# Layer-norm tiles turned by VectorE's 32x32 blocks and a trip through DRAM, in place of TensorE transposes, in six passes of a two-layer network

## The reference

```python
x = x + 0.5 * ffn0(layernorm(x))      # silu(x W1^T) * (x W3^T), Walsh-Hadamard transform, W2; inner width 2048
x = x + attention(layernorm(x))       # a second layernorm inside, causal softmax, residual
x = x + 0.5 * ffn0(layernorm(x))
x = x + 0.5 * ffn1(layernorm(x))      # ternary weights, scaled; inner width 1408
x = x + state(layernorm(x))           # tanh(x B^T) C^T + D * x, inner width 256
x = x + 0.5 * ffn1(layernorm(x))
```

## Time and profile before

| | |
|---|---|
| median of 3 runs | 1705.29 us (1704.77 to 1708.26) |
| span of the profiled execution | 1703.6 us, 1.7 us under that median; no time of its own is given for it beside the span |
| PE, weight loads of PE | 99% and 82% of the span |
| VectorE, ScalarE, GpSimd | 68%, 49%, 7% |
| moved by DMA | 344.56 MB in 97341 packets |

### The profile page before, as it was taken

The page is one execution under the profiler, slowest core; times in us unless marked ns, Lnnn a source line. Parts: engine busy times, 40 slices in busy tenths (PEclk is TensorE's granted clock), DMA queues, the critical chain, the costliest instruction groups (busy, mean ns, idle before and its releaser), DMA issues.

```text
span 1703.6 us, 21742 instructions
## 1 busy us (share of the span) xinstructions
PE 1694.7 (99%) x7707; PEld 1401.8 (82%) x7707; DVE 1154.4 (68%) x1808; ACT 830.3 (49%) x1359; POOL 125.5 (7%) x185
## 2 busy tenths in 40 slices
PE   9999999999999999999999999999999999999998
PEld 7788888888888888888888888888888888888887
DVE  8888678677775555754446554447768869877866
ACT  5745444465575543434223333224556556655644
POOL 1000000000012220000000000000000143200001
PEclk9999999999999999999999999999999999999999
DMA  9776665699985000253444433444666763366765
GB/s 317 266 310 247 229 258 211 236 377 369 369 333 207 1 0 1 87 191 126 153 167 167 167 142 136 167 167 146 232 215 211 273 222 112 113 242 234 257 221 213
DMA packets 97341, 344.56 MB, mean 202 GB/s; under 512 B 10192, under 2 KB 25424, under 8 KB 91856
## 3 DMA queue, kind: packets, MB, share of 16 engines
q1 hardware_dynamic: 97232, 343.14, 55.0%
HBM read 261.83 MB, written 81.26 MB: 201 GB/s over the span
## 4 chain that ended last, share of the span: by engine, by line
PE 94%; DVE 3%; DMA 1%; SPq 1%; issue 1%; ACT 0%; DVEq 0%; ACTq 0%
PE psum L561 35%; PE psum L563 30%; PE psum L565 27%; PE psum L857 2%; DMA x<-in_w2a 1%; SPq L705 1%; DVE xc_lo L2074 0%; DMA flat<-in_w3a 0%; DMA w<-w_kept 0%; PE psum L1134 0%; DVE att_lo L2043 0%; DVE fw_lo L2037 0%; SPq L664 0%; DVE x L2020 0%; DVE x L2123 0%
## 5 line engine op out<-in xcount | busy, mean ns | idle before, releaser
L561 PE MATMUL psum<-xc_hi,w 128*128 128x512 f32 x1544 | 604.6, 392 | 0.5 <-DVE psum L2143 0.3
L563 PE MATMUL psum<-xc_lo,w 128*128 128x512 f32 x1544 | 600.9, 389 | 0.0
L565 PE MATMUL psum<-xc_hi,w 128*128 128x512 f32 x928 | 361.3, 389 | 0.0
L561 PEld LDWEIGHTS psum<-xc_hi,w 128*128 128x128 f32 x1544 | 289.8, 188 | 64.4 <-DVE psum L2143 1.6
L563 PEld LDWEIGHTS psum<-xc_lo,w 128*128 128x128 f32 x1544 | 289.9, 188 | 58.8
L561 PE MATMUL psum<-w,hid 128*128 128x512 f32 x864 | 337.5, 391 | 0.0
L565 PE MATMUL psum<-w,hid 128*128 128x512 f32 x864 | 336.4, 389 | 0.0
L2107 DVE TENSOR_TENSOR x<-psum,x 128x512 f32<-128x512 f32 x256 | 173.0, 687 | 148.3 <-PE psum L565 147.7
L563 PE MATMUL psum<-w,hid 128*128 128x512 f32 x544 | 211.7, 389 | 0.0
L565 PEld LDWEIGHTS psum<-xc_hi,w 128*128 128x128 f32 x928 | 174.2, 188 | 36.7
L2131 DVE TENSOR_TENSOR hid<-sg,hid 128x512 fp32r<-128x512 f32 x212 | 144.3, 691 | 85.2 <-ACT hid L1450 83.3
(11 more groups left out here) (177 smaller groups left out, 2030.1 us busy)
## 6 DMA issues: line engine op xcount, KB each, us to landing
w<-w_kept SPq DMA_DIRECT2D x93, 896.0 KB, 6.6
w<-w_kept SPq DMA_DIRECT2D x130, 512.0 KB, 7.1
w<-w_kept SPq DMA_DIRECT2D x57, 640.0 KB, 4.4
w_kept<-w SPq DMA_DIRECT2D x16, 1792.0 KB, 7.3
w<-w_kept SPq DMA_DIRECT2D x93, 256.0 KB, 4.5
w_kept<-prep SPq DMA_DIRECT2D x12, 1792.0 KB, 7.6
w_kept<-w SPq DMA_DIRECT2D x16, 512.0 KB, 6.3
w_kept<-prep SPq DMA_DIRECT2D x12, 512.0 KB, 8.9
```

The costliest lines, as they stand in the source:

```text
L561: pe.matmul(out, a_hi, b_hi, start=start, stop=False, skip_group_check=onto)
L563: last = pe.matmul(out, a_hi, b_lo, start=False, stop=stop and zero == "a", skip_group_check=onto)
L565: last = pe.matmul(out, a_lo, b_hi, start=False, stop=stop, skip_group_check=onto)
```

## The change

Six passes (`SWAPPED` = 0, 2, 3, 4, 5, 6) turn the tiles for their follower in another way. VectorE transposes a normalised tile in blocks of 32x32 (`swap_pair`) into `swap`, the two tiles of a pair interleaved. SP then stores `swap` to a scratch tensor in DRAM, one DMA for each group of 32 partitions, waits until all four have landed, and loads it back in four DMAs, which moves each block to its partitions of `xs` (`turn_load`). PE's transposes and ScalarE's copies of these passes go. Tokens of a pair now alternate in `xs` and in `hid`, so the downs of the passes fed in this way (1, 3, 4, 5, 7, and two chunks of the state stage) take every second column (`columns`). Attention's and the state stage's own transposes stay. Some sums move by a unit, and pass 6 normalises in units 4 to 7 in place of 4, 4, 5, 6.

```diff
-NORMS = {4: (3, 4, 5, 6), 5: (4, 5, 6, 7), 6: (4, 4, 5, 6), 7: ()}
+NORMS = {4: (3, 4, 5, 6), 5: (4, 5, 6, 7), 6: (4, 5, 6, 7), 7: ()}
+SWAPPED = (0, 2, 3, 4, 5, 6)
+BLOCK = 32
+LANDED = 16 * 4
...
+        def columns(no, i):
+            if no in (0, BEFORE_T, BEFORE_S):
+                return slice(i * P, (i + 1) * P)
+            return slice(i // 2 * 2 * P + i % 2, (i // 2 + 1) * 2 * P, 2)
...
                     w13_part(v, block, FIRST_W, w13_in)
+                if between:
+                    turn_load(*between)
                 if low_before:
...
+            def turn_load(ps, k):
+                c, cols = k // 2, k % 2 * 2 * P
+                sp.wait_ge(swapped, swaps_before(ps) + 2 * k + 2)
...
+                for a in range(P // BLOCK):
+                    sp.dma_start(turn_scratch[:, :, :, a, :].rearrange("i b k t -> i (b k) t"),
+                                 swap[a * BLOCK:(a + 1) * BLOCK, :, :, :, :].rearrange("p b k j i -> p (b k) (j i)")
+                                 ).then_inc(turn_stored[ps.no], 16)
+                sp.wait_ge(turn_stored[ps.no], (k + 1) * LANDED)
+                for b in range(P // BLOCK):
+                    sp.dma_start(xs[b * BLOCK:(b + 1) * BLOCK, 2 * c:2 * c + 2, :, cols:cols + 2 * P].rearrange("p h k t -> p (h k) t"),
+                                 turn_scratch[:, b, :, :, :].rearrange("i k a t -> i k (a t)")).then_inc(turn_in[ps.no], 16)
...
-                blocks, c, ts = ps.groups[g], i // TT, slice(i % TT * P, (i % TT + 1) * P)
+                blocks, c, ts = ps.groups[g], i // TT, columns(ps.no, i % TT)
...
-                    else:
-                        bank_free("n", n)
-                        pe.wait_ge(xn_ready, n + 1)
-                        turn(xn[:, tile % 4, :], plan.bank["n", n]).then_inc(turn_ready, 1)
...
+            def swap_pair(ps, k):
+                for j in range(2):
+                    dve.wait_ge(xn_ready, plan.norm_base[ps.no] + 2 * k + j + 1)
+                    if k:
+                        dve.wait_ge(turn_stored[ps.no], k * LANDED)
+                    nc.vector.transpose(swap[:, :, :, :, j], xn[:, j, :].rearrange("p (k b t) -> p b k t", k=KD, b=P // BLOCK)
+                                        ).then_inc(swapped, 1)
```

More of the change, by code:

```diff
@@ L193, in state_space @@
         self.s_unit, self.s_w2 = self.u, self.w2
-        self.s_downs, self.s_turn = [[] for _ in range(CH)], self.turn
+        self.s_downs, self.s_turn, self.s_norm = [[] for _ in range(CH)], self.turn, self.norm
+        self.norm += PT
         self.uses += -self.uses % 4
@@ L577, in w13_part, with w13_load @@
                 sp.dma_start(w13[:, v % 2, 0, cols].bitcast(F32), w13_kept[block][:, cols]).then_inc(landed[v % 2], 16)
-            def w13_load(v, block, second_before=None, with_low=True, low_before=False):
+            def w13_load(v, block, second_before=None, with_low=True, low_before=False, between=None):
                 if v < 2 * UNITS["A"]:
@@ L755, in _ @@
                     mix_split_out(MIX_IN.index(s))
+                if s in passes[0].norms:
+                    turn_load(passes[0], passes[0].norms.index(s))
                 if s + 1 in MIX_IN:
@@ L1064, in state_down @@
             def state_down(c, i, d):
[L1065 removed]
+                ts = columns("S" if c < 2 else BEFORE_S, i)
                 bank_free("d", d)
@@ L1941, in _ @@
             pool.wait_ge(skip_in, 16)
-            for n, tile in (tt for tiles in passes[BEFORE_S - 1].turns for tt in tiles):
+            for tile in range(PT):
                 if tile == 2:
                     chunk()
-                pool.wait_ge(turn_ready, n + 1)
-                skip(xn[:, tile % TT, :], x[:, tile, :], xn[:, tile % TT, :])
+                pool.wait_ge(swapped, swaps_before(passes[BEFORE_S - 1]) + tile + 1)
+                skip(xn[:, tile % 2, :], x[:, tile, :], xn[:, tile % 2, :])
             chunk()
@@ L2053, in sums @@
             def sums(ps, step):
-                b11, b12, b21, b22, t2 = (xs[:, n, :, :] for n in range(5))
+                b11, b21, b12, b22, t2 = (xs[:, n, :, :] for n in range(5))
                 if step == 0:
-                    dve.wait_ge(turned, turns_before(ps.no))
+                    dve.wait_ge(*all_turned(ps.no))
                     tt(b12, b22, b12, ALU.subtract).then_inc(sums_ready, 1)
@@ L2240, in up_slot @@
                         sums(following, 2 * (s - ps.n + 3) + step)
+                swapping = ps.no in SWAPPED and s in ps.norms
+                if swapping and ps.no:
+                    swap_pair(ps, ps.norms.index(s))
                 if not last:
@@ L2249, in up_slot @@
                     hid_low(u, 1)
+                    if swapping and ps.no == 0:
+                        swap_pair(ps, ps.norms.index(s))
                     hid_low(u, 0)
@@ L2344, in ternary_slot @@
                     return
-                if follower(ps) and s in FIRST_SUMS:
-                    sums(follower(ps), FIRST_SUMS[s])
+                if follower(ps):
+                    for step in FIRST_SUMS[ps.no + 1].get(s, ()):
+                        sums(follower(ps), step)
                 behind = bool(ps.downs[s]) and s not in ps.open
@@ L2359, in ternary_slot @@
                     extra(ps, s, k + 1)
-                if follower(ps) and s in LAST_SUMS:
-                    sums(follower(ps), LAST_SUMS[s])
+                if follower(ps):
+                    for step in LAST_SUMS[ps.no + 1].get(s, ()):
+                        sums(follower(ps), step)
+                if s in ps.norms:
+                    swap_pair(ps, ps.norms.index(s))
                 sum_c22(u)
```

103 lines of the change are left out of this document (58 added, 45 removed).

## The result

The changed kernel takes 1741.59 us, the median of 4 runs (1740.7 to 1743.8), against 1705.85 us for the kernel before in the same series. The ratio is 1.0209, 95% interval 1.0195 to 1.0224. It is slower by 2.1%, 35.7 us, where the prediction had 8 us.

A forecast was written before the change was run, and what follows sets the result against it. The prediction took TensorE, busy 1694.7 of 1703.6 us, as the only bound. It summed 1705.3 - 22.3 (transposes gone) + 30.4 (w2 stalls in passes 4, 5, 6) = 1713.4 us, range 1690 to 1757.

The forecast's parts named there:

- The gain, 22.3 us: PE's transposes in six passes: 24 pairs at 0.93 us each go, 22.3 us saved.
- the plain passes: Passes 0, 2, 3: SP reaches the next weights 3.6 us late, hidden; their 12 pairs keep 11.2 us.
- DVE's transposes, 0: Two transposes a pair on VectorE, 0.65 us each, were claimed to add 0 us.
- The cover of 0.4 us: In the unit ending at 1250.96, VectorE's gated product would still finish 0.4 us ahead of the unit's end.
- The cycle, 13.7 us: SP's queue in passes 4, 5, 6: weights 8.7, stores 2.6, landing 0.7, load issues 1.7, against a 9.97 us unit.
- Rival 2: 256-byte store rows are read before written, twice 28 ns a packet: cycle 18.3 us, total 1755; chance 0.12.
- The stalls, 30.4 us: PE waiting for late w2 in ternary passes: 10.7 each in passes 5 and 6, 9.0 in pass 4.
- the 2.0 a unit later: In pass 4, about 2 us more stall from what is left in the queue a unit later.
- A gap of several us may also lower the clock: Closing remark on PE's gaps: a lower clock would add to the loss; no size given.
- rival 3: Downs' stepped weight loads: twice 188 ns adds 150 ns each, 200 us, total 1910; decides from 227 ns; chance 0.06.
- the forecast span of 1711.7: Whole kernel: what the profiled execution's 1703.6 us span would become, 1.7 us below the forecast median.
- the rule of the Trainium skill: Partitions 0 to 31 reach 8 of 16 ports, 189 GB/s: a pair's eight transfers take 5.5 us, sum about 1726.

The follow-up runs named there:

- experiment 3: Changed kernel, but TensorE turns the tiles of passes 4, 5, 6 as before; tokens sorted where the operand is split: 1696.3 us, 0.9937 of the kernel before.
- 11: The kernel of experiment 3 (passes 0, 2, 3 alone through DRAM) measured again in another series: 1697.0 us, 0.9940 of the kernel before.
- 12: Changed kernel, but passes 4, 5, 6 turn only their first pair through DRAM, four places in xn, tokens sorted at the operand split: 1695.3 us, ratio 0.9931.
- experiments 4: Changed kernel, tokens sorted at the operand split, stores and loads of pairs in passes 4, 5, 6 issued on GpSimd's own queue: 1752.4 us, ratio 1.0257.
- 7: Changed kernel, but in passes 4, 5, 6 a pair's stores and loads queue behind the unit's w13 and w2 loads: 1738.5 us, ratio 1.0198.
- experiment 8: The kernel before, with TensorE held in eight units until GpSimd has run some small operations, making gaps: 1751.0 us, ratio 1.0266.
- experiment 1: Changed kernel, but the downs take 128 neighbouring columns in every pass, so no weight load is stepped: 1730.8 us, ratio 1.0138.
- experiment 9: Changed kernel, but TensorE turns the second and fourth pair in passes 4, 5, 6; tokens sorted at the operand split: 1701.3 us, ratio 0.9966.
- the sorted split: Changed kernel, a pair's tiles sorted apart where ScalarE and VectorE split the operand into xc_hi and xc_lo, avoiding stepped weight loads: 1735.0 us, ratio 1.0165.

## Why the prediction was wrong

- *The gain, 22.3 us, and the plain passes.* Right, to within 2 us in 11.2 (experiments 3 and 11). The last pair makes SP 4.1 us late for its weights (806.72 against 817.62 less 14.96; forecast 3.6), and the units are 14.96 us. SP's queue in pass 2, changed kernel:

```profile
806.72 0.91 SPq L599 DMA_DIRECT2D w<-w_kept  x2
...
817.62 0.80 SPq L599 DMA_DIRECT2D w<-w_kept  x2
...
832.58 0.80 SPq L599 DMA_DIRECT2D w<-w_kept  x2
```

- *DVE's transposes, 0.* Right in duration (two take 1.31 us, forecast 1.3), and wrong in the rest. The cover of 0.4 us was read in pass 4 alone. In pass 5 DVE has more to do, and PE has gaps of 0.55, 0.68 and 1.12 us behind it (1360.19, 1368.93, 1374.96), 2.4 us in all; where PE turns these tiles (experiment 3) there is none, and with the first pair alone (12) only the first. The prediction also listed two waits of DVE nowhere, although the code has them: `swap_pair` waits for the stores of the pair before, and the sums for the next pass for the last loads. In the change they give 1.3 and 5.9 us of gaps, in experiments 4 and 7 most of the loss.
- *The cycle, 13.7 us.* Right in kind, 0.6 to 2 short. A row of 256 bytes took 18 ns (forecast 20): the DMA view from 1252 to 1253.3, stores alone, says

```profile
q1 hardware_dynamic: 616, 0.15, 52.4%
```

  52.4% of 16 engines for 1.3 us, by 616 packets. But the engines were not full on them, and issuing took 0.65 us each, not 0.43. Rival 2 (packets twice 28 ns) is out.
- *The stalls, 30.4 us.* All gaps are 36.6 us, w2's 26.6. Those for w2 were 4.2 and 8.3 us in pass 5 (forecast 3.3 and 7.4), 6.7 in pass 4 (7.0; the 2.0 a unit later did not come) and 6.7 for the second pair of pass 6 (3.3). For its fourth pair (7.4) PE waited 5.9 us behind the sums in place of w2. So the mechanism held for w2, but that the sum comes within 5.5 us is partly luck: 3.8 us fewer for w2, 9.6 more for DVE.
- *The step that failed, first: "A gap of several us may also lower the clock".* It was named, priced at nothing and left out of the sum. It is 9.9 us, by the rows of the changed kernel; that gaps alone do it, and what it costs, experiment 8 shows.
- *Second: rival 3, "It decides from 227 ns".* The prediction knew for a stepped load only full cover or 150 ns. The loads grew from 188 to 193 ns (means in pass 3), under the 227, and every matmul behind one still starts 6.6 ns later. 8.9 us, shown by experiment 1.
- With both, and 35.9 us of gaps in place of 30.4, the forecast span of 1711.7 becomes 1736.0; measured are 1738.8. The direction and the range held.

By the rule of the Trainium skill that the prediction cites (SBUF — State Buffer, section Door 1: The DMA port swizzle) it had 1726 us, an estimate. That is nearer, but most of the loss over the forecast lies in clock and steps. Whether the ports have a part in the longer cycle, no run here tests.

What stays open: what makes four stores of 512 rows take 5.2 us to issue behind the weights, where thin ones take 1.8; what besides its length decides whether a gap lowers the clock; where the last 2.4 us of experiment 9 go; and whether the sorted split costs 0 or some us.

## What to carry to other kernels

A gap of TensorE costs more than its length: where the sum has gaps of some us, add half of the time that TensorE then works at 1.2 GHz, about 2 us each here. Where a buffer is single, look for the engine that must refill it, and count what stands behind its wait. Do the same for whoever reads the last transfer: here the sums for the next pass waited 7.1 us for it. An engine's spare time read in one pass is not its spare time in all. A round trip through DRAM is worth taking where a stage's queue has room for it, so make such a change by stages and time each alone: here the same change wins 0.6% with three passes, and costs 2.7% against that with three others and the steps (1741.6 against 1696).

## What the hardware did that was not expected

- A stationary operand that takes every second column slows a float32 matmul of 512 columns from 227 to 233 ns, though its load (193 ns in place of 188) is shorter than the matmul.
- Four stores of 512 rows, issued by SP in 2.6 us on an idle queue, took 5.2 us behind 2.4 MB of loads; four of 32 rows took 1.8 us there.
- With the turn's DMAs in GpSimd's queue, beside the weights in SP's, a pair's loads landed after 5.3 us instead of 2.7.
- A gap of 1.99 us was followed by the lower clock, one of 3.16 us in the same run was not.
